# V of a window attention computed by head parity in column halves of the array, with scores spread to 64 columns a head

## The reference, cut to what matters

```python
y = _ln(x, norm1_w, norm1_b)
y = jnp.roll(y, (-3, -3), axis=(1, 2))
win = y.reshape(B, 8, 7, 8, 7, C).transpose(0, 1, 3, 2, 4, 5).reshape(B * 64, 49, C)
qkv = (win @ qkv_w.T).reshape(B * 64, 49, 3, 8, 16).transpose(2, 0, 3, 1, 4)
attn = jnp.einsum('bhnd,bhmd->bhnm', q, k) * scale + bias + mask
attn = jax.nn.softmax(attn, axis=-1)
out = jnp.einsum('bhnm,bhmd->bhnd', attn, v) ...
x = shortcut + out @ proj_w.T + proj_b
z = _ln(x, norm2_w, norm2_b)
return x + gelu(z @ fc1_w.T + fc1_b) @ fc2_w.T + fc2_b
```

## Time and profile before

| | |
|---|---|
| median of 3 runs | 5296.85 us (5293.0 to 5299.09) |
| the profiled execution's own time | 5297.13 us |
| its span | 5295.3 us |
| mean granted TensorE clock | 0.98 |
| busy: TensorE, VectorE, ScalarE, GpSimd | 91%, 69%, 64%, 50% |

### The profile page before, as it was taken

The page is one execution under the profiler, slowest core; times in us unless marked ns, Lnnn a source line. Parts: engine busy times, 40 slices in busy tenths (PEclk is TensorE's granted clock), DMA queues, the critical chain, the costliest instruction groups (busy, mean ns, idle before and its releaser), DMA issues.

```text
span 5295.3 us, 197343 instructions
## 1 busy us (share of the span) xinstructions
PE 4843.6 (91%) x73224; PEld 3669.2 (69%) x73224; DVE 3643.9 (69%) x7453; ACT 3405.9 (64%) x5387; POOL 2623.6 (50%) x3763
## 2 busy tenths in 40 slices
PE   3688888599999999999999999999999999999998
PEld 1455566477777777777777777777777777777776
DVE  2233333577777777777777777777777777777775
ACT  1233333377777777777777777777777777777776
POOL 6233333355555555555555555555555555555554
PEclk7899999799999999999999999999999999999999
DMA  2344443100000000000000000000000000000000
GB/s 63 103 130 129 133 130 117 34 26 25 26 26 26 26 26 26 26 25 25 26 26 25 25 26 26 26 26 25 25 25 26 26 26 26 26 26 26 26 25 22
DMA packets 304837, 219.26 MB, mean 41 GB/s; under 512 B 49206, under 2 KB 252008, under 8 KB 304680
## 3 DMA queue, kind: packets, MB, share of 16 engines
q1 hardware_dynamic: 304680, 216.83, 14.0%
HBM read 111.15 MB, written 111.94 MB: 42 GB/s over the span
## 4 chain that ended last, share of the span: by engine, by line
PE 70%; DVE 15%; issue 8%; ACT 3%; SPq 2%; DVEq 1%; POOL 1%; DMA 0%; ACTq 0%; POOLq 0%
PE bank L659 13%; PE bank L651 11%; PE bank L575 9%; DVE xn L1012 8%; PE bank L582 7%; PE bank L592 5%; PE bank L517 5%; PE bank L638 4%; PE bank L567 4%; DVE sc L987 4%; PE bank L530 4%; ACT shared L823 2%; PE bank L605 2%; PE bank L628 2%; PE bank L617 2%
## 5 line engine op out<-in xcount | busy, mean ns | idle before, releaser
L659 PE MATMUL bank<-fc_sb,g 128*98 128x128 f32 x8192 | 998.6, 275 | 1.5 <-ACT g L817 1.5
L659 PEld LDWEIGHTS bank<-fc_sb,g 128*98 128x98 f32 x8192 | 910.2, 165 | 19.8 <-ACT g L817 2.7
L651 PE MATMUL bank<-zt,fc_sb 128*128 128x392 f32 x2048 | 895.0, 519 | 3.0 <-ACT zt L810 2.3
L1153 POOL TENSOR_TENSOR res<-x,projb 98x512 f32<-98x512 f32 x256 | 325.4, 1271 | 1122.2 <-DVE x L1029 1122.2
L1012 DVE TENSOR_SCALAR xn<-x,lnp 98x128 f32<-98x128 f32 x1024 | 838.1, 879 | 4.0 <-POOL lnp L1082 4.0
L1171 POOL TENSOR_TENSOR sc<-sc,mx 128x784 f32<-128x784 f32 x512 | 775.5, 1517 | 11.2 <-DVE mx L993 3.3
L987 DVE TENSOR_TENSOR sc<-bank,shared 128x392 f32<-128x392 f32 x1024 | 528.8, 558 | 324.5 <-PE bank L592 324.4
L817 ACT ACTIVATE g<-bank,fc1b 128x392 f32<-128x392 f32 x1024 | 586.7, 587 | 247.8 <-PE bank L651 244.5
L605 PEld LDWEIGHTS bank<-ident_sb,sc 128*98 128x98 f32 x4096 | 465.2, 127 | 174.7 <-issue 98.1
L1082 POOL TENSOR_TENSOR lnp<-st 98x8 f32<-98x8 f32 x777 | 144.9, 214 | 847.9 <-DVE st L875 847.9
L971 DVE TENSOR_TENSOR shared<-bank,vmask_sb 98x512 f32<-98x512 f32 x512 | 354.0, 691 | 283.0 <-PE bank L575 283.0
(11 more groups left out here) (87 smaller groups left out, 7698.9 us busy)
## 6 DMA issues: line engine op xcount, KB each, us to landing
x<-x_scratch SPq DMA_DIRECT2D x768, 49.0 KB
out_x<-y SPq DMA_DIRECT2D x672, 49.0 KB
xc_even<-in_x SPq DMA_DIRECT2D x128, 196.0 KB
shared<-in_x SPq DMA_DIRECT2D x128, 196.0 KB
x_scratch<-xc_even SPq DMA_DIRECT2D x128, 196.0 KB
x_scratch<-shared SPq DMA_DIRECT2D x128, 196.0 KB
x<-x_scratch SPq DMA_DIRECT2D x256, 38.5 KB
out_x<-y SPq DMA_DIRECT2D x224, 38.5 KB
```

The source lines that it names most:

```text
L651: nc.tensor.matmul(ring[:, 0:ST], fc1[:, 128 * j:128 * j + 128], zt[:], start=True, stop=True).then_inc(full, 1)
L659: mm = nc.tensor.matmul(RC[0:PT, C * p:C * p + C], g[:, c, PT * p:PT * p + PT], fc2[:, c, :], start=c == 0, stop=c == HC - 1)
```

## The change

V is computed by head parity. The host reorders the V columns of the weight, so that all even heads come first (64 columns), then all odd heads. For each window two matmuls with 49 stationary columns and 64 moving ones go to rows 0 to 48 and rows 64 to 112 of one bank, on tiles of 128 rows by 64 columns of the array. All 8 windows fit in `RB[0]`; `RB[1]` is not used for V. VectorE copies rows 0 to 48 into the even half of `vb`, ScalarE rows 64 to 112 into the odd half (right behind `k_out`); both wait for the last matmul of `values` 1. The other half of each row of `vb` stays zero from a memset at the start of the second part. `xt` holds each window once, and `xt_out` writes 392 columns instead of 784. So that the probabilities come out in rows of (parity, token padded to 64), the scores lie 64 columns apart a head, in the banks and in `sc`; `probs_t` transposes 113 columns instead of 98; `row_sums` and `attend` have 113 rows instead of 98. `sc` is cleared once, at the end of `fill`, in place of `mx`; w2's raw weights have a buffer of their own, as `sc` is now larger. The semaphore counts of `b_full` and `b_out` change accordingly.

```diff
-    row = np.arange(PT) // N
-    c["vmask"] = np.broadcast_to((row[:, None, None] == (np.arange(HEADS) % 2)[None, :, None]),
-                                 (PT, HEADS, D)).astype(np.float32).reshape(PT, HEADS * D)
+    row = np.arange(VT)
+    c["vmask"] = np.broadcast_to(((row // QROWS)[:, None, None] == np.arange(2)[None, :, None]) &
+                                 ((row % QROWS)[:, None, None] < N), (VT, 2, D)).astype(np.float32).reshape(VT, 2 * D)
...
-        vb = shared[0:PT, v0:p0].rearrange("p (u w h d) -> p u w h d", u=2, w=WINS, h=HEADS)
-        pt = shared[0:PT, p0:p0 + PAIRS * QUADS * 2 * N].rearrange("p (k q v n) -> p k q v n", k=PAIRS, q=QUADS, v=2)
+        vb = shared[:, v0:p0].rearrange("p (u w q h d) -> p u w q h d", u=2, w=WINS, q=QUADS, h=2)
+        pt = shared[0:VT, p0:p0 + PAIRS * QUADS * 2 * N].rearrange("p (k q v n) -> p k q v n", k=PAIRS, q=QUADS, v=2)
...
-        xt = sb("xt", [C, WINS, 2, N])
+        xt = sb("xt", [C, WINS, N])
-        sc = sb("sc", [128, 2, QUADS, PAIRS, 2, N])
+        sc = sb("sc", [128, 2, QUADS, PAIRS, 2, QROWS])
-        staging = sc[:].rearrange("p u q k h m -> p (u q k h m)")
+        staging = sb("staging", [128, TAPS * HALF])
...
+        def score_bank(q):
+            return bank[q][:].rearrange("r (k h m) -> r k h m", k=PAIRS, h=2)[:, :, :, 0:N]
...
             def values(t, j):
-                wait(pe, b_out[j], b_before(t, j, 0))
-                for w in range(4):
-                    rows = xt[:, 4 * j + w].rearrange("c v n -> c (v n)")
-                    mm = nc.tensor.matmul(RB[j][0:PT, C * w:C * w + C], rows, wqkv[:, 2 * C:3 * C],
-                                          start=True, stop=True)
-                mm.then_inc(b_full[j], 1)
+                if j == 0:
+                    wait(pe, b_out[0], 5 * t.n - 3)
+                for w in range(4 * j, 4 * j + 4):
+                    for hh in range(2):
+                        mm = nc.tensor.matmul(RB[0][QROWS * hh:QROWS * hh + N, 64 * w:64 * w + 64], xt[:, w],
+                                              wqkv[:, 2 * C + 64 * hh:2 * C + 64 * hh + 64], start=True, stop=True)
+                if j == 1:
+                    mm.then_inc(b_full[0], 1)
             def project(t, i):
-                nc.tensor.matmul(RA[:, 0:ST], wqkv[:, C * i:C * i + C], xt[:, :, 0, :],
+                nc.tensor.matmul(RA[:, 0:ST], wqkv[:, C * i:C * i + C], xt[:],
...
-                        mm = nc.tensor.matmul(bank[q][QROWS * v:QROWS * v + QROWS, 2 * N * p:2 * N * p + 2 * N],
+                        mm = nc.tensor.matmul(score_bank(q)[QROWS * v:QROWS * v + QROWS, p],
-                                              km[32 * q:32 * q + 32, w].rearrange("p h m -> p (h m)"),
+                                              km[32 * q:32 * q + 32, w],
...
-                    mm = nc.tensor.transpose(RB[j % 2][0:PT, 128 * q:128 * q + 128],
-                                             sc[:, t.u, q, j].rearrange("p h m -> p (h m)"), ident[:])
+                    mm = nc.tensor.transpose(RB[j % 2][0:VT, 128 * q:128 * q + 128],
+                                             sc[:, t.u, q, j].rearrange("p h m -> p (h m)")[:, 0:VT], ident[:])
             def attend(t, j):
-                                              vb[:, t.u, w, 2 * q:2 * q + 2].rearrange("p h d -> p (h d)"),
+                                              vb[0:VT, t.u, w, q].rearrange("p h d -> p (h d)"),
             def row_sums(t):
-                                          vmask[:, 0:2].rearrange("p h d -> p (h d)"),
+                                          vmask[:],
...
             def xt_out(t):
-                xhat = RA[:, 0:ST].rearrange("c (w n) -> c w n", n=N).unsqueeze(2).to_broadcast([C, WINS, 2, N])
-                nc.scalar.activation(xt[:], xhat, ACT.Identity, scale=ln[:, 0:1], bias=ln[:, 1:2]).then_inc(a_out, 1)
+                nc.scalar.activation(xt[:].rearrange("c w n -> c (w n)"), RA[:, 0:ST], ACT.Identity, scale=ln[:, 0:1],
+                                     bias=ln[:, 1:2]).then_inc(a_out, 1)
+            def v_out(t):
+                act.wait_ge(b_full[0], 4 * t.n - 2 if t.c or not t.fixed else 1)
+                act.wait_ge(vb_clear, 1)
+                nc.scalar.activation(vb[QROWS:VT, t.u, :, :, 1], RB[0][QROWS:VT, :].rearrange(
+                    "p (w q d) -> p w q d", w=WINS, q=QUADS), ACT.Copy).then_inc(b_out[0], 1)
...
             def pt_out(t, j):
-                full_ = RB[j % 2][0:PT, :].rearrange("p (q v n) -> p q v n", q=QUADS, v=2)
+                full_ = RB[j % 2][0:VT, :].rearrange("p (q v n) -> p q v n", q=QUADS, v=2)
             def exponentials(t, r):
-                half_sc = sc[:, t.u, 2 * r:2 * r + 2].rearrange("p q k h m -> p (q k h m)")
+                half_sc = sc[:, t.u, 2 * r:2 * r + 2].rearrange("p q k h m -> p (q k h) m")[:, :, 0:N]
...
+                    v_out(t)
...
-                V.memset(mx[:], 0.0).then_inc(xc_summed, 1)
+                V.memset(sc[:], 0.0).then_inc(xc_summed, 1)
...
+            V.memset(vb, 0.0).then_inc(vb_clear, 1)
+            dve.wait_ge(vb_clear, 1)
...
-            def v_out(t, j):
-                V.tensor_tensor(out=vb[:, t.u, 4 * j:4 * j + 4],
-                                in0=RB[j][0:PT, :].rearrange("p (w h d) -> p w h d", w=4, h=HEADS),
-                                in1=vmask[:].unsqueeze(1).to_broadcast([PT, 4, HEADS, D]),
-                                op=ALU.mult).then_inc(b_out[j], 1)
+            def v_out(t):
+                dve.wait_ge(b_full[0], 4 * t.n - 2 if t.c or not t.fixed else 1)
+                V.tensor_copy(vb[0:N, t.u, :, :, 0], RB[0][0:N, :].rearrange(
+                    "p (w q d) -> p w q d", w=WINS, q=QUADS)).then_inc(b_out[0], 1)
...
-                    V.tensor_tensor(out=sc[:, t.u, q].rearrange("p k h m -> p (k h m)"), in0=bank[q][:, 0:ST],
-                                    in1=b.rearrange("p k h m -> p (k h m)"), op=ALU.add).then_inc(s_out, 1)
+                    V.tensor_tensor(out=sc[:, t.u, q, :, :, 0:N], in0=score_bank(q), in1=b,
+                                    op=ALU.add).then_inc(s_out, 1)
             def maxima(t, r):
-                             sc[:, t.u, 2 * r:2 * r + 2].rearrange("p q k h m -> p (q k h) m"),
+                             sc[:, t.u, 2 * r:2 * r + 2].rearrange("p q k h m -> p (q k h) m")[:, :, 0:N],
...
             def strips(t):
-                    v_out(t, 0)
-                if t.there():
-                    v_out(t, 1)
+                    v_out(t)
...
+    v_cols = arrays["qkv_wT"][:, 2 * C:].reshape(C, QUADS, 2, D).transpose(0, 2, 1, 3).reshape(C, C)
+    arrays["qkv_wT"] = np.ascontiguousarray(np.concatenate([arrays["qkv_wT"][:, :2 * C], v_cols], 1))
```

More of the change, by code:

```diff
@@ L18 @@
 PT = 2 * N
+VT = 64 + N
 ST = WINS * N
@@ L164, in program @@
         headmask = sb("headmask_sb", [C, 2])
-        vmask = sb("vmask_sb", [PT, HEADS, D])
+        vmask = sb("vmask_sb", [VT, 2 * D])
         winmask = sb("winmask_sb", [128, 2, PAIRS, N])
@@ L238, in program @@
         A_JOBS = 3
-        B_JOBS = (4, 5)
-        SUMS, PROJECTION = 3, 4
+        SUMS, PROJECTION = 2, 3
         SMALL = 6
@@ L269, in program, with after_v, full0, out0 @@
         CONV_LOADS, BIAS_LOADS, LOADS = [], [], []
[L271 to L275, removed]
+        def after_v(t):
+            return 1 if t.back(-1).there() else 0
+        def full0(t, job):
+            return 4 * t.n + job + after_v(t)
+        def out0(t, job):
+            return 5 * t.n + 1 + job + 2 * after_v(t)
+        def score_bank(q):
+            return bank[q][:].rearrange("r (k h m) -> r k h m", k=PAIRS, h=2)[:, :, :, 0:N]
         block_ = ctx.enter_context(nc.Block())
@@ L357, in _ @@
             load(headmask[:], a["headmask"])
-            load(vmask[:], a["vmask"].rearrange("p (h d) -> p h d", h=HEADS))
+            load(vmask[:], a["vmask"])
             load(winmask[:].rearrange("p a k m -> p (a k m)"), a["winmask"])
@@ L602, in probs_t @@
                     pe.wait_ge(exp_done, 2 * t.n + 2)
-                wait(pe, b_out[j % 2], b_before(t, j % 2, 1 + j // 2))
+                wait(pe, b_out[j % 2], out0(t, 1 + j // 2) if j % 2 == 0 else 4 * t.n + j // 2)
                 for q in range(QUADS):
-                    mm = nc.tensor.transpose(RB[j % 2][0:PT, 128 * q:128 * q + 128],
-                                             sc[:, t.u, q, j].rearrange("p h m -> p (h m)"), ident[:])
+                    mm = nc.tensor.transpose(RB[j % 2][0:VT, 128 * q:128 * q + 128],
+                                             sc[:, t.u, q, j].rearrange("p h m -> p (h m)")[:, 0:VT], ident[:])
                 mm.then_inc(b_full[j % 2], 1)
             def attend(t, j):
-                wait(pe, b_out[0], b_before(t, 0, 3))
-                wait(pe, b_out[1], b_before(t, 1, 2 + j))
+                wait(pe, b_out[0], out0(t, 3))
+                wait(pe, b_out[1], 4 * t.n + 1 + j)
                 for w in range(4 * j, 4 * j + 4):
```

(22 more changed lines are left out.)

11 lines of the change are left out of this document (5 added, 6 removed).

## The result

The changed kernel takes 5323.36 us (median of 5 runs, 5316.73 to 5327.02) against 5296.85 before (5 runs): a ratio of 1.0051, 95% interval 1.0036 to 1.0066, so 26.5 us slower where 30 faster were forecast. The profiled execution is the one of 5327.02 us, with a span of 5325.2 and a granted clock of 0.98 as before.

The account below looks back on a forecast made before the run. Alternating TensorE and VectorE paths bound the strips; gains of 0.10 and 0.17 us, mean 0.135 times 256, give 35 us, less 5 for memsets: 5297 - 30 = 5267 us. Range 5240 to 5330, the forecast's own 5240 to 5284.

Parts of the forecast that it names:

- What bounds the kernel: Attention strips, 16.67 us on average: TensorE and VectorE paths of nearly one length alternate; GpSimd's second subtract sets the xn end.
- V on TensorE: V matmuls: column halves overlap, so a half strip takes 0.79 us against 0.88, 0.17 less a strip.
- the 0.33 of a visit to the tiled form: V on TensorE: leaving the whole-array form and returning costs 0.33 us per half, the middle of 0.29 and 0.37.
- ScalarE's copy: Between k_out and the gelus' table load: 0.39 us, bounded by 0.33 and 0.59, leaving 0.10 of the 0.17 gain.
- ScalarE takes the gain: Rival: the copy costs 0.59 us, delaying gelu 0 and hidden 2; 5294, no change. Chance 0.14.
- Hidden edits: xt_out, project, bank waits, wider transposes, spread scores on VectorE and SP's queue: nothing, project to 0.02 us a strip.
- GpSimd on the spread scores: Rival: the subtract slows to 1.94 us on spread scores, +0.34 a strip, 5389. Chance 0.10.
- Halves of V in turn: Rival: V's column halves do not overlap, a half costs 1.25 us, 0.74 more a strip, 5491. Chance 0.04.
- scores into a gapped bank: Rival: score matmuls writing PSUM with gaps take double, 0.51 us more a strip, 5432. Chance 0.04.
- Once: Memsets of sc and vb, 3.4 and 1.7 us with nothing beside them: +5 us, ends 2 and 6.

Follow-up runs that it names:

- experiment 8: The kernel before with only GpSimd's residual2 moved from behind the subtracts to ahead of the factors: 5272.61 us, ratio 0.9951.
- experiment 7: The changed kernel with ScalarE's copy of V behind gelu 0 and GpSimd's residual2 moved ahead of the factors: 5219.5 us, ratio 0.9853 to the kernel before.
- experiment 1: The changed kernel with ScalarE's copy of V moved from right behind k_out to behind gelu 0: 5244.07 us, ratio 0.9904 to the kernel before.
- Experiment 6: The changed kernel with ScalarE's copy of V, in its place, cut to 256 of 512 columns: 5269.93 us, ratio 0.9945 to the kernel before.
- experiment 4: The kernel before with only the scores spread to 64 columns a head, V still masked over the whole array: 5296.04 us, ratio 1.0006.
- against 2: The changed kernel with ScalarE's copy of V, in its place, cut to 16 of 512 columns: 5246.99 us, ratio 0.9907 to the kernel before.

## Why the prediction was wrong

**What bounds the kernel: right.** Two paths of nearly one length, TensorE's 16.58 and VectorE's 16.75 (experiment 8); the last `xn` held up by GpSimd's residual (experiments 7 and 8).

**V on TensorE: right.** A half is 0.59 in the chain plus 0.87 - 0.67 = 0.20 that the K passes behind it take more: 0.79, as worked out, against 0.88. TensorE's path shortens by 0.21 (16.58 to 16.37, experiments 8 and 7), 0.17 forecast; VectorE's by 0.19 (16.75 to 16.56, experiment 1). What the 0.33 of a visit to the tiled form consists of, no run separates.

**ScalarE's copy: the step that failed.** "0.39 us" rests on 256 columns. One parity of V is eight windows of 64 channels, 512 columns, as the diff shows, and they take 593 ns; by the prediction's own slope of 0.86 ns a column from the `qt` row, 512 columns would have given 0.61. That is 0.20 of the error. A further 0.10 is the overlap that the prediction took over from the two `km` activations (two of 587 in 1.07): the copy began 0.02 after `k_out` ended, and the table load 0.03 after the copy. Together 0.31 with 0.01 for the gaps: `hidden` 2 comes 0.21 later than before and not 0.10 earlier. Experiment 6, with 256 columns, shows the two terms apart: with the size as assumed the kernel is 27 us faster than before, near the forecast's 30. TensorE's strip then gains 0.02 instead of 0.10, which is the overlap missing, and the other strip 0.19.

**The rival came in, and its price was too low.** "ScalarE takes the gain" named this mechanism and even the 0.59, but gave 5294. It counted 0.10 too little again (the overlap), and let VectorE's strip keep 0.15. Every strip passes gelu 0 and `hidden` 2, so the TensorE path of 16.58 + 0.20 = 16.78 is the longer one in both: one strip loses 0.20, the other 0.03 instead of gaining 0.15. Their mean is 0.115, as measured. The copy's bound of 0.59 in the range was put into this rival alone, at 0.14; with the columns counted rightly it was the likeliest case. The range of 5240 to 5330 holds the time all the same, near its upper end.

**Hidden edits: right.** Bias, scores and the shorter `xt_out` have no effect on the end (experiment 4 for the layout). VectorE's copy is 682 ns and not the 410 forecast, the same miscount, but it is still shorter than the two masked products of 691, and it has slack. **GpSimd on the spread scores**: 1537 ns, where 1940 were feared. **Halves of V in turn** and **scores into a gapped bank**: neither came; the run of 16 V passes lasts 0.59, and the time of experiment 4 excludes the second. The Trainium skill, "PSUM — Partial Sum Buffer", Specifications, has non-contiguous patterns slow matmuls significantly; experiment 4 does not show it for runs of 49 in 64.

**Once: the terms right, their effect not shown.** The two memsets last 3.47 and 1.76 us in the trace after, as forecast. But the first bias of the second part starts at 994.43 us there, at 990.83 in the trace before, at 988.81 in that of experiment 7, which has both memsets, and at 1001.69 in that of experiment 8, which has neither. The first part differs from one profiled execution to the next by more than the memsets take, so no run shows that they cost time. From that bias to the end the changed kernel takes 4330.8 us and the one before 4304.5: 26.3 more, which with the 3.6 ahead of it makes the 29.9 between the two profiled executions. The strips alone would give 29; the first three intervals between strips, which are of other lengths, are together 2.3 shorter after the change.

## What to carry to other kernels

Before work is moved to an engine with idle time, count its elements from the access pattern in the diff, and look at what is queued behind the new place: 0.59 us in front of the one activation that TensorE waits for cost all of the gain and more, while 0.59 us one instruction later cost nothing that the time shows (experiment 1 against 2). Where two paths alternate, a delay on a stretch that both kinds of strip pass must be set against both lengths, and the longer one counts in every strip. And a slow instruction on one engine can be another's doing: VectorE's `xn` became fast when GpSimd did its residual earlier.

## What was not expected of the hardware

- VectorE's `xn` (98x128) last 883 ns on average in experiment 1 and 640 in experiment 7, while `z` of the same form stays at 335. The means mix long and short ones. These are the last three of a strip in the trace before (start us, us, engine, what), beside the subtracts and the residual of the earlier trace rows:

```profile
3014.24 1.53 DVE L1012 TENSOR_SCALAR xn<-x,lnp 98x128 f32<-98x128 f32 x1
3015.68 1.31 DVE L1012 TENSOR_SCALAR xn<-x,lnp 98x128 f32<-98x128 f32 x1
3016.92 0.34 DVE L1012 TENSOR_SCALAR xn<-x,lnp 98x128 f32<-98x128 f32 x1
```

  The first of these starts inside the second subtract and ends 0.08 us behind it, the next starts inside the residual and ends 0.09 behind that, and the last starts as the residual ends. It is so from 2000 to 5000 us of this trace: 360 of 721 `xn` start well inside such a GpSimd instruction and end 0.08 to 0.09 us behind it, and the other 361, which start in its last 0.2 us or behind it, last 0.34. The maximum (`mx`) keeps its 0.97 us inside a subtract. In experiments 7 and 8 no residual stands behind the subtract, and three of four `xn` are short. The VectorE program is unchanged there (worth 24.8 us in experiment 8, and by the ratios of 1 and 7 another 27 there).
- Activations on ScalarE overlap or not depending on the pair: the two of `km`, 587 ns each, start to end in 1.07 us, but the copy behind them begins 0.02 us after their end, the table load 0.03 us after the copy's. A gelu behind the copy in experiment 1 does not overlap it either (copy from 3001.16 to 3001.75, gelu at 3001.78). A copy of 49 rows costs 593 ns for 512 columns, 380 for 256, 178 for 16: on average 0.84 ns a column over some 165 ns.
- The weight load's record of a transpose grows from 127 to 177 ns with 113 columns instead of 98, and nothing in the time shows it (experiment 4).
